# A fused convolution, attention and expert kernel: attention queries in 7 chunks of 448 in place of 8 of 392, and the pool engine's second additions deferred by a round

## The reference

```python
x = x + conv3x3(groupnorm(x), sign(weight))            # 64 -> 64 channels
t = tokens(x)                                          # 3136 tokens of 64 channels per image
t = t + attention(layernorm(t))                        # one head, 32 wide, own residual, W_o, b_o
t = t + experts(layernorm(t))                          # 8 experts, gates: softmax of the batch mean at each position
```

## Time and profile before

| | |
|---|---|
| median of three runs | 7050.26 us |
| profiled execution, its own time | 7055.03 us |
| its span | 7053.2 us |
| mean granted TensorE clock | 0.986 of full speed |
| PE busy | 6827.4 us, 97% of the span |
| DVE busy | 5077.8 us, 72% |
| ACT busy | 4355.5 us, 62% |
| POOL busy | 5472.6 us, 78% |

### The profile page before, as it was taken

How to read it: one execution, slowest core, us unless ns; L and a number is a source line. 1 busy time by engine, 2 the same in 40 slices (tenths; PEclk the granted TensorE clock), 3 DMA queues, 4 the chain that set the end, 5 groups by cost and what they waited for, 6 DMA issues and landing times. The chain is left out here.

```text
span 7053.2 us, 132108 instructions
## 1 busy us (share of the span) xinstructions
PE 6827.4 (97%) x50610; PEld 3615.0 (51%) x50610; DVE 5077.8 (72%) x9184; ACT 4355.5 (62%) x9296; POOL 5472.6 (78%) x5522
## 2 busy tenths in 40 slices
PE   6999999999999999999999999999999997999999
PEld 3555555555555555555555555555555553333333
DVE  6777777777777777777777777777777762655565
ACT  1666666666666666666666666666666664555555
POOL 2888888888888888888888888888888895222222
PEclk7999999999999999999999999999999997999999
DMA  1111111111111111111111111111111002444443
GB/s 31 15 24 24 24 24 24 24 24 24 24 24 24 24 24 24 24 24 24 20 19 24 24 24 24 24 24 24 24 24 24 10 10 56 100 101 103 101 102 93
DMA packets 328980, 248.83 MB, mean 35 GB/s; under 512 B 253672, under 2 KB 311408, under 8 KB 324256
## 3 DMA queue, kind: packets, MB, share of 16 engines
q1 hardware_dynamic: 316064, 214.68, 13.7%
q0 software_dynamic: 12288, 25.71, 1.8%
HBM read 162.70 MB, written 77.59 MB: 34 GB/s over the span
## 5 line engine op out<-in xcount | busy, mean ns | idle before, releaser
L618 ACT ACTIVATE probs<-bank 128x392 f32<-128x392 f32 x6400 | 2796.9, 496 | 1887.0 <-PE bank L667 1841.0
L481 DVE TENSOR_REDUCE part_max<-bank 128x1 f32<-128x448 f32 x5600 | 3213.3, 614 | 583.9 <-PE bank L660 573.8
L660 PE MATMUL bank<-ks,qs 96*128 96x448 f32 x5600 | 2347.9, 424 | 55.3 <-DVE part_max L481 50.0
L428 POOL TENSOR_TENSOR psum<-psum,probs 128x392 f32<-128x392 f32 x2048 | 2098.6, 1025 | 318.3 <-ACT probs L618 33.1
L425 POOL TENSOR_TENSOR psum<-probs 128x392 f32<-128x392 f32 x2048 | 2099.5, 1025 | 240.9 <-ACT probs L618 229.5
L667 PE MATMUL bank<-qs,ks 97*128 97x392 f32 x6400 | 2027.4, 367 | 15.6 <-ACT probs L618 13.3
L676 PE MATMUL bank<-probs,vs 128*32 128x392 f32 x12288 | 1768.2, 507 | 34.1 <-POOL psum L428 26.6
L678 PE MATMUL bank<-psum,ones 128*32 128x392 f32 x4096 | 1740.7, 507 | 0.0
L660 PEld LDWEIGHTS bank<-ks,qs 96*128 96x128 f32 x5600 | 1065.5, 190 | 1230.8 <-DVE part_max L481 745.5
L667 PEld LDWEIGHTS bank<-qs,ks 97*128 97x128 f32 x6400 | 1191.7, 190 | 407.0 <-ACT probs L618 223.0
L985 ACT ACTIVATE h<-l_bank,xin 128x392 f32<-128x392 f32 x1024 | 639.0, 674 | 445.1 <-PE l_bank L1079 445.1
(11 more groups left out here) (126 smaller groups left out, 5740.3 us busy)
## 6 DMA issues: line engine op xcount, KB each, us to landing
xin<-in_x_dram SPq DMA_DIRECT2D x64, 784.0 KB, 8.9
xs<-x_dram SPq DMA_DIRECT2D x512, 98.0 KB, 2.5
xpk<-in_x_dram SPq DMA_DIRECT2D x64, 392.0 KB, 12.6
t_dram<-t SPq DMA_DIRECT2D x32, 784.0 KB, 5.3
x_dram<-xn SPq DMA_DIRECT2D x32, 784.0 KB, 6.9
res<-t_dram SPq DMA_DIRECT2D x256, 98.0 KB, 2.7
out_dram<-fin POOLq DMA_DIRECT2D x256, 98.0 KB, 2.8
gate_w<-gate_dram SPq DMA_DIRECT2D x16, 392.0 KB, 5.2
```

The lines of the kernel that those rows point to most:

```text
L428: add = gp.tensor_tensor(into, into, three, ALU.add)
L481: v.tensor_reduce(part_max[:, b, m:m + 1], m_bank[place.bank()][:, 0:MW], AX.X, ALU.max).then_inc(m_used, 1)
L618: s.activation(probs[:, held(c, k), :], s_bank[n % 3][:, 0:2 * QW], ACT.Exp, scale=SCALE).then_inc(p_ready, 1)
L660: mm(m_bank[place.bank()][:, 0:MW], qs[par][0:KS, b * P:(b + 1) * P], ks[par][0:KS, m * MW:(m + 1) * MW], start=True, stop=True).then_inc( ...
```

## The change

The queries are cut into 7 chunks of 448, so that an image has 175 scores of 448 columns, 56 rounds and 56 value visits. The second addition of a round, and the small one of the 25th block, become entries of their own in the list, each one round later: POOL does the first addition of the next round and then the second of this one. `qs` keeps the queries in their natural order; a score matmul reads two pieces of 224 from the two halves of the image, and the maxima's query blocks are taken in an order (`BLOCK_OF`) in which one transfer serves both halves. All places of the list are set anew. `psum` holds 6 rounds in place of 8. Value visits stand 3.38 places earlier relative to their round.

```diff
-QC = 8
+QC = 7
-HELD, SUMS = 16, 8
+HELD, SUMS = 16, 6
-VISIT_AT, DOOR = 0.0, 1
-SUM_LAG, APPLY_LAG = 1.22, 3.72
-GATHER_AFTER, DIVIDE_AFTER, DIVIDE_STEP = -0.19, 0.1, 0.73
-STATS_AT, STATS_STEP, PAD_AT, PAD_STEP = 93.6, 2.18, 117.81, 17.71
+VISIT_AT, DOOR = -3.38, 1
+SUM_LAG, APPLY_LAG = -0.53, 3.66
+GATHER_AFTER, DIVIDE_AFTER, DIVIDE_STEP = -0.07, 0.1, 0.89
+STATS_AT, STATS_STEP, PAD_AT, PAD_STEP = 66.71, 2.02, 106.86, 10.5
...
-BORDER, LAST_MAX = 58.0, 9.34
+BORDER, LAST_MAX = 50.76, 8.77
...
         for r in range(ROUNDS):
-            order.append((c * BLOCKS + GROUP * (r + 1) - 0.5 + SUM_LAG, "attend", "sum", (c, r)))
+            at = c * BLOCKS + GROUP * (r + 1) - 0.5 + SUM_LAG
+            order.append((at, "attend", "sum", (c, r)))
+            for kind, later in (("third", GROUP + 0.1), ("tail", GROUP - 0.2))[:1 + (r + 1 == ROUNDS)]:
+                at += later
+                order.append((at, "attend", kind, (c, r)) if at < SLOT else (at - SLOT, "norms", kind, (c, r)))
...
-    return -(-(c + 1) * 2 * QW // (P * MR))
+    return c + 1
+BLOCK_OF = [b + d for b in range(0, KB // 2, 2) for d in (0, 1, KB // 2, KB // 2 + 1)] + [KB - 1]
...
-ACT_LAG = 0.9
+ACT_LAG = 0.14
...
-            if n < 2:
-                return tile[part, 0:S].rearrange("p (c a i) -> p c a i", a=2, i=QW)[:, q * CW // QW:(q + 1) * CW // QW, n, :]
-            return tile[part, (n - 2) * HALF + q * CW:(n - 2) * HALF + (q + 1) * CW]
+            return tile[part, n % 2 * HALF + q * CW:n % 2 * HALF + (q + 1) * CW]
...
-                        gp.wait_ge(p_ready, im.count(QC * KB, first + 3))
-                        gp.wait_ge(sum_part, im.count(QC * (ROUNDS + 1), rounds + c + 1))
-                        add = gp.tensor_tensor(into, into, three, ALU.add)
-                        if r + 1 == ROUNDS:
...
+                        elif kind == "third":
+                            gp.wait_ge(p_ready, im.count(QC * KB, first + 3))
+                            gp.wait_ge(sum_part, im.count(QC * ROUNDS, rounds + 1))
+                            gp.tensor_tensor(into, into, three, ALU.add).then_inc(sum_ready if r + 1 < ROUNDS else round_part, 1)
+                        else:
+                            rest = slice(0, S - BLOCKS * P)
+                            gp.wait_ge(p_ready, im.count(QC * KB, first + 4))
+                            gp.wait_ge(round_part, im.count(QC, c + 1))
+                            gp.tensor_tensor(into[rest], into[rest], probs[rest, HELD, :], ALU.add).then_inc(sum_ready, 1)
...
-                        mm(s_bank[(c * KB + k) % 3][:, 0:2 * QW], ks[par][0:KS + 1, k * P:(k + 1) * P], qs[par][0:KS + 1, c * 2 * QW:(c + 1) * 2 * QW],
+                        queries = qs[par][0:KS + 1, 0:S].rearrange("p (a n) -> p a n", a=2)[:, :, c * QW:(c + 1) * QW]
+                        mm(s_bank[n % 3][:, 0:2 * QW].rearrange("p (a n) -> p a n", a=2), ks[par][0:KS + 1, k * P:(k + 1) * P], queries,
                            start=True, stop=True).then_inc(s_done, 1)
```

More of the change, by code:

```diff
@@ L369, in step @@
                         blocks = slice(r * MR, min((r + 1) * MR, KB))
-                        n0, n1 = blocks.start * P, min(blocks.stop * P, S)
                         sp.wait_ge(rowmax_ready, im.count(NMR, r + 1))
@@ L418, in step @@
                         gp.wait_ge(pad_lo, im.count(CH, r + 1))
-                    elif kind == "sum":
+                    elif kind in ("sum", "third", "tail"):
                         c, r = a
                         first, rounds = c * KB + GROUP * r, c * ROUNDS + r
-                        one, two, three = (probs[:, held(c, GROUP * r + n), :] for n in range(GROUP))
-                        into = psum[:, rounds % SUMS, :]
-                        gp.wait_ge(p_ready, im.count(QC * KB, first + 2))
-                        gp.tensor_tensor(into, one, two, ALU.add).then_inc(sum_part, 1)
-                        gp.wait_ge(p_ready, im.count(QC * KB, first + 3))
-                        gp.wait_ge(sum_part, im.count(QC * (ROUNDS + 1), rounds + c + 1))
-                        add = gp.tensor_tensor(into, into, three, ALU.add)
-                        if r + 1 == ROUNDS:
-                            add.then_inc(sum_part, 1)
+                        one, two, three = (probs[:, held(im, c, GROUP * r + n), :] for n in range(GROUP))
+                        into = psum[:, im.count(QC * ROUNDS, rounds) % SUMS, :]
+                        if kind == "sum":
+                            gp.wait_ge(p_ready, im.count(QC * KB, first + 2))
+                            gp.tensor_tensor(into, one, two, ALU.add).then_inc(sum_part, 1)
+                        elif kind == "third":
+                            gp.wait_ge(p_ready, im.count(QC * KB, first + 3))
+                            gp.wait_ge(sum_part, im.count(QC * ROUNDS, rounds + 1))
+                            gp.tensor_tensor(into, into, three, ALU.add).then_inc(sum_ready if r + 1 < ROUNDS else round_part, 1)
+                        else:
+                            rest = slice(0, S - BLOCKS * P)
@@ L615, in step @@
                         c, k = a
-                        n = c * KB + k
-                        act.wait_ge(s_done, im.count(QC * KB, n + 1))
-                        s.activation(probs[:, held(c, k), :], s_bank[n % 3][:, 0:2 * QW], ACT.Exp, scale=SCALE).then_inc(p_ready, 1)
+                        n = im.count(QC * KB, c * KB + k)
+                        act.wait_ge(s_done, n + 1)
+                        s.activation(probs[:, held(im, c, k), :], s_bank[n % 3][:, 0:2 * QW], ACT.Exp, scale=SCALE).then_inc(p_ready, 1)
                     elif kind == "gather":
```

42 lines of the change are left out of this document (20 added, 22 removed).

## The result

The changed kernel takes 7204.7 us (median of 4 runs, 7200.9 to 7207.1) against 7052.7 for the kernel before in the same comparison: ratio 1.0211, interval 1.0198 to 1.0224. It is 2.1% slower. Forecast were 6930 us, a range of 6840 to 7015 and 0.09 for slower: wrong in sign, and out of the range by 190 us.

The account below looks back on a forecast made before the run. PE was taken to bound the attention phase. Per image -3.05 + 0.2 - 0.6 = -3.45 us, 107 us over 31 images, plus 15 for the last, took 7055 to 6933, stated as 6930 us, range 6840 to 7015.

Parts of the forecast that it names:

- Visits: PE's value visits: 64 become 56 per image with the same columns, saving 0.33 us each, 2.64 us.
- scores: PE's score matmuls: 200 of 0.18 us become 175 of 0.205, taken as -0.42 us per image.
- two pieces: Queries read as two pieces of 224 per score: 0 to 1.6 us per image, taken as 0.2.
- the 3.05 us: PE's counted matmul time per image falls from 171.7 to 168.7 us, -3.05.
- Addition: POOL's addition of 448 columns: 1.125 us, upper end 1.170; starts 1.08 us apart, POOL about 151 us busy per image.
- Last image: Image paced by POOL, without maxima beside it: seven chunks of 19.3 us in place of eight of 19.0, 15 us taken.
- the one headed DVE: DVE's load from denser maxima and divisions: 83% before and 85% after in a dense chunk.
- -0.6: Net slack change per image: +0.6 for fourth maxima, -1.0 for fewer dense chunks, with POOL's 0.2.
- slack time: Lateness per image beyond the counted matmul distances: 8.2 us before; ends after the change 5 to 13 us.
- -1.0 for one dense chunk less: Slack saved per image by four and a half dense chunks in place of five and a half, 1 us each.
- DVE decides: Rival: DVE cannot follow the denser maxima, each dense chunk loses 1 us more; 7070 us, chance 0.09.
- the fixed part stays: Rival: wider visits pay their switch in proportion, only the last image's 15 us remain; 7040 us, chance 0.04.

Follow-up runs that it names:

- e6: e1 with BORDER 53.6 in place of 50.76, so the next image's first maximum stands later in PE's order: 7009 us, ratio 0.9938.
- e14: e6 with reciprocals of 8 columns in place of 112, the other inverses being 1: 6871 us, ratio 0.9746.
- e13: Kernel before with reciprocals of 8 columns in place of 98, the other inverses being 1: 7014 us, ratio 0.9950.
- e1: Changed kernel with the group norm's shift gb computed by ACT from a negated mean, not by DVE: 7100 us, ratio 1.0077.
- e8: Kernel before with the second additions deferred and the shift gb on ACT: 7008 us, ratio 0.9938.
- e10: e6 with divisions spread (DIVIDE_STEP 1.25 in place of 0.89) and three sums moved 2.4 to 3.7 places later: 6983 us, ratio 0.9900.
- e16: e10 with the third variance of the preparation 1.3 places later: 6980 us, ratio 0.9901.
- e2: Changed kernel with each second addition directly behind its first again, so no deferral: 7174 us, ratio 1.0180.
- e3: Kernel before with the deferral of the second additions alone: 7018 us, ratio 0.9962.
- e15: e10 with the shortened reciprocals of e14: 6924 us, ratio 0.9824.

## Why the prediction was wrong

*Visits, scores, two pieces: right.* A round of four maxima after, from visit to visit, takes 2.53 us (2873.63 to 2876.16) against 2.39 in the earlier trace rows; 56 more columns in two sweeps and three scores are 0.12 us, the rest rounding. No round shows a price for the second piece. A kernel of seven chunks with neither of the two misplacements (e6) is at 179.0 us an image, and 174.6 with a short division (e14). Eight chunks with the short division (e13) stand at 178.9, but without the deferral, and short of POOL; eight chunks with deferral, shift on ACT and short division were not run. So the distances between matmuls bear the 3.05 us out, and no pair of times does by itself.

*Addition: right.* 1.142 us (taken 1.125, upper 1.170), starts 1.08 to 1.12 us apart, POOL busy for 155 us an image (taken: about 151). PE's waits for POOL's sums fell from 34.0 us over the run (26.6 for L428, 7.4 for L434) to 16.7 (8.5 and 8.2), as forecast. But this sum treated the 0.14 us bubbles as loss; that DVE's `gb` got in there, it did not see.

*Last image: 12.5 us from the last `m` to the end, forecast 15, near by luck.* Its chunks take 20.5 us (123.1 / 6), not 19.3, so that by this sum 8 x 19.0 - 7 x 20.5 = 8.5 us are won. The stretch from the last `m` also holds another image's maxima, and why the two differ was not followed up.

*The failed step is the one headed DVE, and its sum "-0.6" for the slack time.* Taken were 7.6 us an image, with 13 as the upper end; measured 16.6. It asked only whether DVE has time for its instructions, by their durations before. Four things were missing:
- An instruction counted at nothing, since in the kernel before it lasted 0.15 us. Its duration depended on where POOL stood. 99 to 105 us (e1), or 31 x 3.35.
- The first maximum's distance from the last projection, to be read from `BORDER` and `PROJ_AT` in the change: 90 us (e6), a balance with maxima that moved as well.
- The clock. The count prices every matmul at the higher level; after, it fell behind both of these waits (a mean of 0.976 in place of 0.986). Up to 80 us of the run are this, and they are inside the 105 and the 90. Where the long waits are gone (e6) it is at 0.987.
- The division's rounds. The prediction took -1.0 for one dense chunk less. (By its own 140 maxima and 27 a chunk, that is 5.2 chunks and not five and a half, so -0.7.) But e6, free of the three above, keeps 10.3 us where e8, eight chunks with the deferral and the shift on ACT, has 7.2: the 3.1 us that the matmuls save are lost again, and 7009 equals 7008. e14 shows how much of DVE's time is in it: with the reciprocals cut, 4.4 us an image go. But e13 shows that the rounds of eight chunks hold 3.7 us of it as well, against 5.4, so some 1.7 of the 3.1 are put down to the divisions by these runs. The rest is open.

So the rival "DVE decides" had the right engine and sign; its price (7070) was for the divisions' rounds alone, and its place (maxima late in most rounds of the dense part) was not the main one. The two misplacements, with the clock, make up 195 us and leave 7009. The last 79 us to 6930 are slack time that stayed, 10.3 us an image and not 7.6; that the divisions' rounds hold them is argued, and e10 wins back 26.

A slip in the rivals: "the fixed part stays" gives 7050 - 15 = 7035, not 7040.

The best kernels here that compute the whole, e16 and e10 (6980 and 6983, 1.0% under before), have seven chunks, the deferral, the shift on ACT, the later first maximum, and spread divisions with the sums behind them.

## What to carry to other kernels

A short duration in a trace can be short because of a gap in another engine's queue. Before gaps are closed or places moved, list the instructions of DVE that read two tensors in SBUF, and rewrite them with a pointer or move them; here there were two in every image, and each became long in some kernel. When an order is rescaled, check the distance of each producer from its first reader in the new order, not only the engines' sums; and when one engine's shortage is cured, ask who is next, as POOL was in e13. When a wait grows, look at the granted clock behind it, and count its fall with the wait.

## What was not expected of the hardware

A DVE instruction with two tensor inputs in SBUF, one element per partition, lasted 3.84 us (median of 32) in place of 0.15 while POOL ran additions end to end. In the 27 images where it was this long it ended 0.02 us behind the end of POOL's run, not of the addition during which it began. With POOL's bubbles of 0.14 us in place it waited for one addition at most: 0.65 us in e2. But without a gap it can get in too: 0.54 us in e3, at the end of the first addition. `mv<-mv` shows both as well. In e15 it was passed over at such an end and lasted 2.02 us; in e6 it ended at one (0.86 us, the next instruction of POOL starting 0.04 us earlier). In no trace, in images 4 to 31, did either last beyond an end with a pause of 0.08 us or more behind it. With one tensor and a pointer `gb` took 0.20 us beside the same additions. Of the two-tensor instructions with one of them in PSUM, `gsq<-bank,gm` lasted 0.16 us at the same place:

```profile
2873.00 0.16 DVE L514 TENSOR_TENSOR gsq<-bank,gm 128x1 f32<-128x1 f32 x1
```

The Trainium skill, SBUF — State Buffer, section "SBUF: two separate sides", has an exclusive lock of a port pair between GpSimd and a DVE instruction with two SBUF inputs, held for a whole instruction. The traces agree on who is kept out, and on its length where there are bubbles and in e3. They differ for `gb` in the changed kernel and `mv` in e15: the wait was for up to four of POOL's instructions, not for one. What decides between the two stays open.
